# Load and first attention as one flat pipeline over the batches, with queries and keys stacked by DMA and probabilities turned by DMA

## The reference

```
q = layernorm(x) @ Wq      # 32 heads of 16 columns
k, v = ctx @ Wk, ctx @ Wv  # 8 kv heads of 16 columns, each serves 4 heads
p = softmax(q k^T / 4)     # 128 x 128 per head and batch
x = x + (p v) @ Wo
```

## Time and profile before

| | us |
|---|---|
| median of 3 runs (1884.77 to 1889.16) | 1888.47 |
| the profiled execution's own time | 1886.01 |
| its span | 1884.3 |
| PE, DVE, ACT, POOL busy | 1605.5, 1178.5, 796.8, 608.8 |
| first instruction of the load | 0.8 |
| first maximum of the first attention (L800) | 51.4 |
| last statistics of the first attention | 270.6 |
| first instruction of stage 1 | 272.4 |

### The profile page before, as it was taken

One profiled execution on the slowest core, in us unless ns is written; L12 is line 12 of the kernel. 1 busy time (PEld: TensorE's weight loads), 2 busy tenths in 40 slices (PEclk: granted clock), 3 DMA queues, 4 the chain that ended last, 5 costly groups with the idle time before them and its releaser, 6 DMA issues. The chain is left out here.

```text
span 1884.3 us, 31640 instructions
## 1 busy us (share of the span) xinstructions
PE 1605.5 (85%) x10796; PEld 897.1 (48%) x10796; DVE 1178.5 (63%) x2287; ACT 796.8 (42%) x2789; POOL 608.8 (32%) x517
## 2 busy tenths in 40 slices
PE   2888955899899999996699999999996769449997
PEld 1455532344366666652365555555552334234443
DVE  5677776434455555564588887888777879771212
ACT  2676755211044334332176666666652312251111
POOL 2333328100014443450066666666653001220000
PEclk9899976799999999998799999999999779869998
DMA  2000012000034442240264546565433000200001
GB/s 103 15 15 15 1 69 92 0 0 0 1 83 93 78 78 62 57 79 26 94 141 104 132 106 129 105 133 107 99 77 91 34 1 1 62 31 0 0 0 45
DMA packets 265956, 111.07 MB, mean 59 GB/s; under 512 B 232305, under 2 KB 248497, under 8 KB 265698
## 3 DMA queue, kind: packets, MB, share of 16 engines
q1 hardware_dynamic: 265826, 109.40, 25.1%
HBM read 52.74 MB, written 2.10 MB: 29 GB/s over the span
## 5 line engine op out<-in xcount | busy, mean ns | idle before, releaser
L67 PE MATMUL bank<-a_wo_hi,a_o_hi 128*128 128x512 f16 (+1 forms) x416 | 159.1, 382 | 19.1 <-DVE a_o_lo L824 10.4
L1443 POOL TENSOR_TENSOR a_recip<-a_total,minus_one 128x4 f32<-128x4 f32 x96 | 97.8, 1019 | 195.9 <-ACT a_probs L1295 195.9
L69 PE MATMUL bank<-a_wo_hi,a_o_lo 128*128 128x512 f16 (+1 forms) x416 | 159.1, 383 | 0.0
L68 PE MATMUL bank<-a_wo_lo,a_o_hi 128*128 128x512 f16 (+1 forms) x416 | 159.1, 382 | 0.0
L1450 POOL TENSOR_TENSOR a_normal<-a_probs,a_recip 128x512 f32<-128x512 f32 x128 | 155.4, 1224 | 7.5
L1435 POOL TENSOR_TENSOR a_q_ss<-a_q_ss,half 128x4 f32<-128x4 f32 x64 | 89.2, 1393 | 189.3 <-DVE a_q_ss L1365 95.5
L1295 ACT ACTIVATE a_probs<-a_masked,a_negmax 128x128 f32<-128x128 f32 x256 | 99.6, 390 | 94.8 <-DVE a_negmax L1340 94.8
L1306 ACT ACTIVATE a_o_hi<-bank 128x512 f16<-128x512 f32 (+1 forms) x96 | 57.1, 595 | 180.6 <-PE bank L69 180.4
L1558 ACT ACTIVATE f_h_hi<-f_h 128x512 f16<-128x512 f32 (+1 forms) x50 | 31.5, 630 | 205.8 <-DVE f_h L1579 144.1
L67 PE MATMUL bank<-xn_hi,f_w_hi 128*128 (+1 forms) x288 | 110.9, 385 | 8.2 <-PEq L1511 8.2
L437 POOL TENSOR_TENSOR a_kb_lo<-a_k_lo,a_spread 128x1024 f16<-128x1024 f16 x32 | 69.4, 2169 | 150.1 <-PE bank L69 139.5
(11 more groups left out here) (338 smaller groups left out, 4894.4 us busy)
## 6 DMA issues: line engine op xcount, KB each, us to landing
a_nq<-in_L_xattn_Wq SPq DMA_DIRECT2D x8, 1024.0 KB, 5.7
a_no<-in_L_xattn_Wo SPq DMA_DIRECT2D x8, 1024.0 KB, 6.0
f_n<-in_L_ffn_w SPq DMA_DIRECT2D x1, 3584.0 KB, 11.6
f_n<-in_L_ffn_w2t SPq DMA_DIRECT2D x1, 3584.0 KB, 20.2
a_nq<-in_L_xattn_Wq SPq DMA_DIRECT2D x4, 768.0 KB, 4.8
a_no<-in_L_xattn_Wo SPq DMA_DIRECT2D x4, 768.0 KB, 5.7
f_words<-in_L_ffn_w SPq DMA_DIRECT2D x2, 1280.0 KB, 6.0
ctx_nat<-in_ctx_t SPq DMA_DIRECT2D x4, 512.0 KB, 4.9
```

Of the source, the lines that this page charges most:

```text
L67: pe.matmul(out, lh, rh, start=start, stop=False)
L68: pe.matmul(out, lh, rl, start=False, stop=False)
L69: return pe.matmul(out, ll, rh, start=False, stop=stop)
L1443: pool.tensor_tensor(recip[s % 2][:, :], total[s % 2][:, :], K.minus_one[:, :], ALU.pow).then_inc(recip_done.sem, 1)
```

## The change

Load and first attention become one function, `first_attention`, written out without a loop, over steps t from -15 to 89. There is one unit per (batch, quarter): unit t belongs to batch t // 8, and holds 4 heads of 128x128 scores, 64 units in all. Each kind of work has an offset in steps (`NORM = -15` ... `ADD = 26`), and each engine walks the steps and does what falls on them in a written order.

What differs within it:

- x and the context are loaded batch by batch (256 KB each), the weights in whole matrices, all through SP; the constant table `keep` is a new input, and the columns of Wq are ordered anew on the host.
- The normalised rows are split in their own layout (DVE copies the high half, POOL subtracts), and turned by a DMA transpose of 128x1024 float16. The same is done with the heads before the multiplication by Wo, and with the probabilities of each unit: 8 + 8 + 64 DMA transposes.
- The keys are masked once per batch (`masked_keys`, DVE, 128x256). Queries and keys are then stacked: 12 DMAs per batch each (4 groups of 32 rows, 3 copies) write high, low, high of the queries and high, high, low of the keys below each other into 96 rows, so that one matmul of 256 columns forms the three products at once. A unit takes two such matmuls.
- Exponentials are taken without row sums (4 per unit); a column of ones beside the values gives the sums in the mixing matmuls (17 columns).
- The high half of the probabilities is a DVE copy from SBUF to SBUF, the low half a POOL subtraction; neither PSUM nor TensorE is in the turning.
- x is added to once per batch (8 times), with the full 512 columns of the heads.

```diff
+    NORM, XHI, XLO, CTX = -15, -15, -13, -12
+    QPROJ, QSPLIT, KPROJ, KMASK, KSPLIT, VPROJ, VSPLIT = -9, -5, -10, -8, -8, -4, -3
+    PHI, PLO, MIX = 2, 2, 7
+    DIVIDE, OSPLIT, OUT, ADD = 11, 17, 22, 26
+    FIRST, END = -15, TOTAL + ADD
...
+    PS, PB = 6, 10
...
+                def scored(b):
+                    if b >= 2:
+                        last = (b - 2) * UNITS + UNITS - 1
+                        sp.wait_ge(s_bank.filled(last), s_bank.n_filled(last))
...
+                def stack_queries(b):
+                    sp.wait_ge(q_bank.freed(b), q_bank.n_drained(b))
+                    scored(b)
+                    for m in range(4):
+                        for third, half in enumerate((0, 1, 0)):
+                            sp.dma_start(q3[b % 2][32 * third:32 * third + 32, m, :, :].rearrange("p g n -> p (g n)"),
+                                         q_hl[b % 2][32 * m:32 * m + 32, half, :]).then_inc(q3_in[b % 2], 16)
...
+                def turn_probs(t):
+                    sp.wait_ge(plo_done.sem, plo_done.count(t))
+                    if t >= PB:
+                        sp.wait_ge(mixed.sem, mixed.count(t - PB))
+                    sp.dma_start_transpose(p_t[t % PB][:, :, :, :].rearrange("p a h n -> p (a h) n"),
+                                           p_hl[t % PS][:, :, :].rearrange("p a n -> p (a n)")).then_inc(p_in[t % PB], 16)
...
+                for t in range(FIRST, END):
+                    for b in at(t, XLO):
+                        turn_queries_in(b)
+                    for b in at(t, KSPLIT):
+                        stack_keys(b)
...
+                    for u in live(t - PLO):
+                        turn_probs(u)
+                    for b in at(t, OSPLIT):
+                        turn_heads(b)
+                    for b in at(t, QSPLIT):
+                        stack_queries(b)
...
+                def mix(t):
+                    b, i, hf = t // UNITS, t % 4, t % UNITS // 4
+                    pe.wait_ge(p_in[t % PB], 16 * (t // PB + 1))
...
+                def exponentials(t):
+                    act.wait_ge(max_done.sem, max_done.count(t))
+                    if t >= PS:
+                        act.wait_ge(plo_done.sem, plo_done.count(t - PS))
...
+                def high_of_probs(t):
+                    dve.wait_ge(s_bank.freed(t), s_bank.n_drained(t))
+                    if t >= PS:
+                        dve.wait_ge(p_in[(t - PS) % PB], 16 * ((t - PS) // PB + 1))
+                    dve.tensor_copy(p_hl[t % PS][:, 0, :], probs[t % PS][:, :]).then_inc(phi_done.sem, 1)
...
+                def low_of_probs(t):
+                    pool.wait_ge(phi_done.sem, phi_done.count(t))
+                    pool.tensor_tensor(p_hl[t % PS][:, 1, :], probs[t % PS][:, :], p_hl[t % PS][:, 0, :],
+                                       ALU.subtract).then_inc(plo_done.sem, 1)
...
-        load_and_split_context(K, a["x"], a["ctx_t"])
...
-    attention(K, A0, *(a[f"L0_xattn_{w}"] for w in ("Wq", "Wk", "Wv", "Wo")))
+    first_attention(K, a["x"], a["ctx_t"], a["keep"], *(a[f"L0_xattn_{w}"] for w in ("Wq", "Wk", "Wv", "Wo")))
```

More of the change, by code:

```diff
@@ L104, in end_stage @@
         self.in_use = []
[L107 to L148, removed]
 class LayerNorm:
@@ L264, in attention @@
         pair = lambda n, shape: (sb(n + "_hi", shape, F16), sb(n + "_lo", shape, F16))
+        ring_of = lambda n, k, shape, dt: [sb(f"{n}{i}", shape, dt) for i in range(k)]
         sem = lambda n: K.sem(f"{N}_{n}")
[L267 to L294, removed]
@@ new lines, in first_attention @@
+        units, batches, halves = list(range(TOTAL)), list(range(B)), [(b, hf) for b in range(B) for hf in range(2)]
+        take = lambda name, banks, uses: Banks(K, f"{N}_{name}", banks, uses)
+        s_bank, o_bank = take("s", K.bank[0:3], units), take("o", K.bank[3:5], halves)
+        q_bank, y_bank = take("q", K.bank[5:6], batches), take("y", K.bank[6:7], batches)
+        kv_bank = take("kv", K.bank[7:8], [(kind, b) for b in batches for kind in "kv"])
+        x_here, ctx_here = [sem(f"x_in{b}") for b in batches], [sem(f"ctx_in{b}") for b in batches]
@@ L441, in attention, with landed @@
+        def landed(engine, sems, b, n=1):
+            engine.wait_ge(sems[b % 2], 16 * n * (b // 2 + 1))
+        def weight(use):
+            kind, i = use
+            if kind == "wo":
+                piece = lambda t: t[:, i, :]
+            elif kind == "wq":
+                piece = lambda t: t[:, :, i * P:(i + 1) * P]
+            else:
+                piece = lambda t: t[:, :, :]
+            return [piece(p) for p in w_p[kind]], piece(nat[kind])
         with nc.Block() as block:
@@ L535, in turned_queries @@
-                def turned_queries(g, use):
-                    b = use[1]
-                    normalised(g, ("qn", b), use)
-                    for h in range(A.heads):
-                        m = pe.transpose(ring[use][:, h * P:(h + 1) * P], qn[:, b % 2, h, :], K.ident[:, :])
-                    return m
-                makers = {"kn": keys_by_row,
-                          "k": turned_keys if A.normed else keys, "v": values, "q": turned_queries if A.normed else queries,
-                          "qn": queries_by_row}
@@ new lines, in _ @@
+                for t in range(FIRST, END):
+                    for u in live(t):
+                        scores(u)
+                    for u in live(t - MIX):
+                        mix(u)
+                    for k in range(KT):
+                        for b in at(t, OUT + k):
+                            project_out(b, k)
+                    for i in range(4):
+                        for b in at(t, QPROJ + i):
+                            queries(b, i)
+                    for b in at(t, VPROJ):
+                        values(b)
+                    for b in at(t, KPROJ):
+                        keys(b)
```

883 lines of the change are left out of this document (342 added, 541 removed), and 4 rows, old and new, of the table A1.

## The result

The change makes the kernel slower: 1895.20 us in the median of 20 runs (1888.72 to 1898.83), against 1887.53 for the kernel before in 20 runs beside it. The ratio is 1.004, with an interval of 1.0032 to 1.0049: a small loss of 0.4%, but clear of the noise. The forecast was 1844, faster. The profiled execution took 1895.11 us with a span of 1893.4.

The account below looks back on a forecast made before the run. SP's issues were to bound the new first attention at 24.4 us per batch; stage 1 at 219, with friction 227 to 228, against 272.4. 1886.0 less 44.4 is 1841.6, plus 2.5 gives 1844; own range 1832 to 1856, wider 1820 to 1882.

Parts of the forecast that it names:

- SP's second term: SP's issue time for 24 stacking DMAs per batch in the new first attention: 0.41 us each, 9.8 us.
- The upper bound: Dearest stacking issue considered for SP: 0.57 us, like loads among transposes, giving 28.3 us per batch.
- rival (a): Stacking DMAs cost SP 0.57 us each, as large loads do: 31 us more, 1874; chance 0.15.
- the friction of 8: Allowance of 8 us over the stage for probability turns queued behind stacking bursts on SP.
- Middle: From the first turn of probabilities to the last query stack: SP's transposes, stacking DMAs and loads, 151 us.
- rival (d): Rings don't decouple; SP idles each batch, then bursts while others idle: 31.4 us per batch, 1892; chance 0.12.
- Ramp: From the first load of x through the queries' stacking to the first turn of probabilities: about 31 us.
- Tail: The last 14 units without stacking, then the last chain through Wo to stage 1: 219, with friction 227 to 228.
- SP becomes the bound: SP, idle before, sets the first attention's pace at 24.4 us per batch; others have 5 to 9 us slack.
- Rival (b): DVE, not SP, sets the pace at 20 us per batch with some waits: 1815 to 1825; chance 0.09.
- Rival (c): DVE's copies wait up to 0.73 us for POOL's subtractions at the port lock: 27 us per batch, 1863; chance 0.19.
- Nothing behind the stage changes: Code after the first attention keeps its time; stage 1 starts from a PE as idle as before.

Follow-up runs that it names:

- masked keys: Against the kernel after: no stacks, keys masked over all eight kv heads, three matmuls of 128 rows and 512 columns per unit; 1803.60 us, ratio 0.9556.

## Why the prediction was wrong

The step that failed is SP's second term, "I take 0.41, because the small loads are nearest in size". The rows were of loads from DRAM; a copy from SBUF costs SP 0.59 in the median and 0.63 to 0.66 with what lies between two, from 1 KB to 128 KB. I chose by bytes where, for copies of the same shape, the source decides (0.42 against 0.59). The upper bound, 0.57 from the loads among transposes, was too low as well, so rival (a) had the right mechanism with too small a price.

Term by term, with the forecast's own marks:

| | forecast | measured |
|---|---|---|
| first turn of probabilities | 31 | 43.9 |
| from there to the end of the last query stack | 151 | 194.0 |
| from there to stage 1, with the friction of 8 | 45 | 36.5 |
| stage 1 begins | 227 | 274.4 |

- Middle, 43 us. 156 stacking issues at 0.66 are 103 us where 66 stood: 37. The rest, 6, lies in the turns, some of them stretched (the longest to 2.33 us) while SP waits for POOL: this is the friction that I had counted at the end. It is 1 us per batch by this difference and 2 by the view of waits (12.6 us). By the stretch at 109 us it comes from the wait for the stack (rival (d)'s place), and not from the depth of the rings.
- Ramp, 13 us. I put only the queries' burst into the chain. In SP's written order the keys' burst of batch 0 (15.43), the rows of batch 1 and the keys' burst of batch 1 (34.27), with six loads around it, stand before the first turn. Of the 13, 36 issues at 0.63 in place of 12 at 0.41 would be 18, part of it hidden. The first maximum stands at 35.0, forecast 28.
- Tail: 36.5 against 37. Right.
- Other engines: DVE 14.2 per batch (15.2), POOL 13.7 (12), DMA engines 17.5 (17 to 19), the transpose 1.29 to 1.31 us long at a pitch of 1.35 (1.33). PE at the lower level "for part of it": 0.68. Right, and none of it mattered.
- "SP becomes the bound": right, shown by 0.61 us in the stage per issue taken away (0.67 by the medians), by no change from fewer bytes, deeper rings or another engine for the high halves, and by the gain when SP is relieved.
- Rival (b), DVE's pace: not reached while stacks stay; DVE is the bound at last with masked keys.
- Rival (c), the port: its 0.73 us set the 1.16 of one line against the 0.43 of another; the line's own operation takes 0.54 in the median of 24, so the row shows 0.62. In the kernel after DVE's copies do go to 582 ns in the mean against 395 at the least, and to 883 when POOL is full, where 0.43 stood. The Trainium skill, "SBUF — State Buffer", section "SBUF: two separate sides", says that the two share ports under a lock; the trace agrees with longer copies beside POOL, though no run isolates the lock. But the price is only paid where DVE or POOL is on the path: 0 us after the change, 10.2 us with masked keys (which also moves 8 copies off a full DVE, so the two are not separated).
- Rival (d), slower: its outcome came (the pace passed 30 us), by the price of (a) and not by its own mechanism.
- "Nothing behind the stage changes": wrong by 7.1 us in the profiles and, as 7.7 in the medians less 2.0 in the stage, by about 5.7. The rotated network makes 3.1 of it. What picks its longer duration stays open: a delay does not bring it to the kernel before, with one delay the kernel after shows the short one and with another the long one, and it may differ from execution to execution.

In sum: 274.4 against the 228.0 of the sum is 46.4 us in the stage, 5.7 come behind it, and the kernel before has its median 0.9 lower in 20 runs than in the three: 51.2, and the miss is 1895.2 - 1844 = 51.2. It closes because the 5.7 is a remainder; by the profiles it is 7.1.

## What to carry to other kernels

Price a DMA for the engine that issues it by its source and kind, from a row of the same kind, and not by its size; where no such row exists, the range has to go well past the nearest one. Many small DMAs on the queue of one engine are work like any other: count them, and look whether a matmul on masked or unstacked data does without them. An edit that brings nothing beside one bound (the high halves on ACT) can bring something beside the next (10.2 us here), so try it again when the bound has moved.

## What the runs showed that I had not expected

- Issue of a plain DMA: 0.42 us from DRAM, 0.59 from SBUF on SP, 0.61 on ACT, 0.50 on POOL (both from SBUF). On SP the size did not matter, from 1 to 128 KB out of SBUF and from 32 to 128 KB out of DRAM. The Trainium skill, "DMA: Bandwidth & Descriptors", section "Issuing engines are not separate DMA queues", says that spreading issues over engines only saves the time to initiate them, which is "usually small relative to the DMA itself". Here an issue took 0.59 us and its landing 1.8, and yet that time, summed over 192 issues on one engine, was the bound: with both stacks off SP the kernel took 57 us less.
- PE's granted clock was 0.64 while it worked 24.5 of 25 us on scores of 32 rows, and 1.00 at 20.6 of 25 with 128 rows and matmuls of 512 columns. The runs differ in rows, in columns of one matmul and in a semaphore per unit; which of these counts was not tried.
- The same code of the rotated network has two durations, 59.9 to 60.7 and 63.7 to 63.9 us.
